# Context's rotated keys and values for the second cross-attention made earlier and kept in DRAM

## What is computed

```python
def _L1_xattn_ref(x, latents, gamma_x, beta_x, gamma_l, beta_l, Wq, Wkv, Wo):
    # x is the context (ctx_1024), latents the decoder's own tokens
    xn = layer_norm(x, gamma_x, beta_x)
    ln = layer_norm(latents, gamma_l, beta_l)
    q = (ln @ Wq).reshape(b, m, h, d)            # 8 heads of 64
    kv_x = xn @ Wkv                              # 256 -> 512 keys, 512 values
    k_x, v_x = (kv_x[..., :INNER], kv_x[..., INNER:])
    kv_l = ln @ Wkv
    ...
    k_x = rope_rotate_k(k_x)                     # k * cos + neg_half(k) * sin
    ...
    k = jnp.concatenate([k_x, k_l], axis=2)
    v = jnp.concatenate([v_x, v_l], axis=2)
    attn = jax.nn.softmax(jnp.einsum('bhid,bhjd->bhij', q, k), axis=-1)
    out = jnp.einsum('bhij,bhjd->bhid', attn, v)
    return out @ Wo
```

## Time and profile before

| | us |
|---|---|
| median of 3 runs | 1689.41 (1687.66 to 1691.91) |
| the profiled execution | 1690.37 |
| its span in the trace | 1688.5 |
| PE busy | 1427.5 (85%) |
| DVE busy | 891.1 (53%) |
| ACT busy | 583.3 (35%) |
| POOL busy | 537.5 (32%) |

### The profile page before, as it was taken

One profiled execution on the slowest core, in us unless ns is written; L12 is line 12 of the kernel. 1 busy time (PEld: TensorE's weight loads), 2 busy tenths in 40 slices (PEclk: granted clock), 3 DMA queues, 4 the chain that ended last, 5 costly groups with the idle time before them and its releaser, 6 DMA issues.

```text
span 1688.5 us, 29289 instructions
## 1 busy us (share of the span) xinstructions
PE 1427.5 (85%) x10056; PEld 1105.6 (65%) x10056; DVE 891.1 (53%) x2529; ACT 583.3 (35%) x1449; POOL 537.5 (32%) x515
## 2 busy tenths in 40 slices
PE   7667997559999999937999589998887766999987
PEld 4454676449999999914666446565555534999975
DVE  7353556531222211169875245767678842666656
ACT  4203543112121222123343124444444212666652
POOL 2002000012222223102333211134435473766775
PEclk9988999669999999977999889999999898999999
DMA  7771000068888888311000061112223699666528
GB/s 224 200 243 51 2 14 14 25 239 326 323 305 311 321 307 319 143 50 50 1 1 1 25 154 35 66 48 88 88 82 104 223 325 330 170 177 174 165 70 339
DMA packets 133602, 258.94 MB, mean 153 GB/s; under 512 B 13898, under 2 KB 106216, under 8 KB 127184
## 3 DMA queue, kind: packets, MB, share of 16 engines
q1 hardware_dynamic: 111328, 210.89, 37.7%
q0 software_dynamic: 17520, 39.88, 6.6%
q10 hardware_dynamic: 4608, 6.29, 1.1%
HBM read 197.71 MB, written 52.72 MB: 148 GB/s over the span
## 4 chain that ended last, share of the span: by engine, by line
PE 50%; issue 8%; DVE 8%; POOL 6%; DMA 5%; SPq 2%; ACT 1%; POOLq 1%; ACTq 0%; DVEq 0%
PE bank L152 46%; POOL xe L1664 4%; DMA arena<-in_banka 2%; PE bank L2208 2%; DMA arena<-yr 2%; DVE arena L1962 1%; PE bank L1079 1%; SPq L2415 1%; DVE arena L1952 1%; DVE arena L197 1%; PE bank L1233 1%; POOLq L165 1%; DVE arena L177 1%; DMA arena<-xd,arena 0%; POOL arena L190 0%
## 5 line engine op out<-in xcount | busy, mean ns | idle before, releaser
L152 PE MATMUL bank<-arena 128*128 128x128 f32 (+8 forms) x8728 | 1282.2, 336 | 149.0 <-DMA arena<-in_banka 24.4
L152 PEld LDWEIGHTS bank<-arena 128*128 128x128 f32 (+5 forms) x8728 | 962.1, 181 | 422.1 <-issue 262.0
L2349 POOL DMA_INDIRECT yr<-arena x159 | 173.3, 1090 | 89.2 <-ACT arena L2279 50.0
L1124 DVE TENSOR_SCALAR arena<-bank,arena 128x128 f32<-128x128 f32 x188 | 52.9, 344 | 279.6 <-PE bank L152 279.6
L190 POOL TENSOR_TENSOR arena<-arena 128x1 f32<-128x1 f32 (+1 forms) x48 | 37.3, 777 | 335.4 <-DVE arena L182 335.4
L1151 POOL DMA_INDIRECT arena<-xd,arena x47 | 45.8, 975 | 257.0 <-PE bank L1079 221.8
L1664 POOL DMA_INDIRECT xe<-arena x112 | 113.2, 1010 | 31.6 <-issue 31.6
L2314 DVE COPY arena<-arena 128x768 f32 x127 | 75.6, 595 | 56.8 <-issue 56.7
L1864 ACT ACTIVATE arena<-bank,arena 128x256 f32<-128x256 f32 x128 | 58.9, 472 | 97.5 <-DVE arena L1952 97.5
L1102 ACT ACTIVATE arena<-bank 128x256 f32<-128x256 f32 x47 | 18.0, 383 | 212.4 <-PE bank L152 212.4
L1111 ACT ACTIVATE arena<-bank,arena 128x128 f32<-128x128 f32 x188 | 53.6, 368 | 92.6 <-PE bank L152 92.6
(11 more groups left out here) (259 smaller groups left out, 1448.2 us busy)
## 6 DMA issues: line engine op xcount, KB each, us to landing
arena<-in_bank SPq DMA_DIRECT2D x47, 2052.0 KB
arena<-xe SPq DMA_DIRECT2D x159, 129.0 KB, 2.4
arena<-kd SPq DMA_DIRECT2D x16, 1024.0 KB, 11.0
arena<-arena SPq DMA_DIRECT2D x16, 896.0 KB, 4.4
arena<-in_bank SPq DMA_DIRECT2D x8, 1536.0 KB, 12.7
arena<-yr SPq DMA_DIRECT2D x16, 768.0 KB, 15.2
xe<-arena SPq DMA_DIRECT2D x1, 6321.0 KB, 29.0
arena<-in_ctx SPq DMA_DIRECT2D x8, 512.0 KB, 4.2
```

Of the source, the lines that this page charges most:

```text
L152: return t.matmul(o, l, r, start=start, stop=stop, skip_group_check=True)
L1124: h = v.tensor_scalar(h_ring[i % 3][:, (4 + m) * 128:(5 + m) * 128], banks[b][:, m * 128:(m + 1) * 128], sbc(w_ring[i % 5], 4100 + m), 0.0 ...
L2349: p.indirect_dma_start(yr, bass.IndirectOffsetOnAxis(ap=sidx.bitcast(I32)[:, n:n + 1], axis=0), y2_ring[n % NY], None, bounds_check=14335, ...
```

## The change

The context's keys and values for all 16 blocks are made before the second cross-attention: blocks 8 to 15 in turns 9 to 17 and in the end of the first cross-attention (that stage still holds context groups 2 and 3), blocks 0 to 7 among the steps of the mixer's first part (their context is loaded again and normalized during the first experts, turns 30 to 33 of DVE's list). Each block's 128x1024 result goes to a DRAM tensor `kxv` from ACT's queue, and the second cross-attention loads it back from SP's queue into a ring of three. The steps are `cn`, `cnd`, `cp` (norm and transposes), `ck` (keys), `cv` (values) and `ct` (transposes of the rotated keys). ACT now copies keys, values and transposed keys; POOL does the whole rotation, in three instructions. The steps `cnorm`, `cnormed`, `pc`, `kx`, `kv0` and `kt` of the second cross-attention are gone. `MIXER` is a new order also for steps that were there (group 1's `sum`, `xa`, `na` and `aff` now come before `0wo`). The core of the diff:

```diff
+        kxv = nc.dram_tensor("kxv", [2048, 1024], F32, kind="Internal").ap()
+        def tensor_kv(t, u, n, bank_of):
+            cT, i, keys, _, _ = kv_place(n)
+            if u == "ct":
+                t.wait_ge(roped, kv_turn(n) + 1)
+                b = bank_of(("ct", n))
+                for m in range(4):
+                    h = t.transpose(banks[b][:, m * 128:(m + 1) * 128], keys[:, m * 128:(m + 1) * 128], ident)
+            else:
...
+                for kc in range(2):
+                    h = mm(t, banks[b], cT[:, kc * 512 + i * 128:kc * 512 + i * 128 + 128], wcol("kv2", kc, 512 if u == "cv" else 0, 512), kc == 0, kc == 1)
+        def scalar_kv(a, u, n):
...
+            if u == "ck":
...
+                a.activation(keys, banks[b], ACT.Copy).then_inc(bank_free[b], 1)
+            else:
+                if n % 8 >= 2:
+                    a.wait_ge(kept[n % 2], 16 * (kv_turn(n) // 2))
+                a.wait_ge(bank_full[b], k + 1)
+                a.activation(both[:, 512:1024] if u == "cv" else both[:, 0:512], banks[b], ACT.Copy).then_inc(bank_free[b], 1)
+                if u == "ct":
...
+                    a.dma_start(kxv[n * 128:(n + 1) * 128, :], both).then_inc(kept[n % 2], 16)
+        def gpsimd_kv(p, n):
...
+            p.wait_ge(bank_free[b], k + 1)
+            p.tensor_tensor(view(part, 0, [[64, 8], [32, 2], [1, 32]]), view(keys, 32, [[64, 8], [-32, 2], [1, 32]]), view(cc("sin"), 0, [[0, 8], [32, 2], [1, 32]]), ALU.mult).then_inc(pstep.up(), 1)
+            p.wait_ge(pstep.sem, pstep.n)
+            p.tensor_tensor(view(keys, 0, [[64, 8], [1, 64]]), view(keys, 0, [[64, 8], [1, 64]]), view(cc("cos"), 0, [[0, 8], [1, 64]]), ALU.mult).then_inc(pstep.up(), 1)
+            p.wait_ge(pstep.sem, pstep.n)
+            p.tensor_tensor(keys, keys, part, ALU.add).then_inc(roped, 1)
...
+            context = [("ck", 8), ("cv", 8)]
+            for n in range(9, 16):
+                context += [("ck", n), ("ct", n - 1), ("cv", n)]
+            context += [("ct", 15)]
+            ln = {9: (("cn", 2),), 10: (("cnd", 2),), 11: (("cn", 3),), 12: (("cnd", 3), ("cp0", 2), ("cp1", 2)), 13: (("cp0", 3), ("cp1", 3))}
...
+                yield from itertools.islice(more, {13: 1, 14: 2, 15: 2, 16: 2, 17: 1}.get(b, 0))
                 if b < 16:
                     yield "mt", b
+                yield from itertools.islice(more, {13: 1, 14: 2, 15: 2, 16: 2, 17: 1}.get(b, 0))
...
+            after = {("ow1", 3): 2, ("lg", 2): 3, ("lg", 3): 3}
...
         def sync_bank(s):
+            for i in range(2):
+                s.wait_ge(kept[i], 64)
...
-            before = {0: ("xnorm",), 1: ("xnormed", "pl0"), 2: ("pl1", "cnorm"), 3: ("cnormed", "pc0"), 4: ("pc1", "qk0"), 5: ("qk1",), 6: ("qk2",), 7: ("qk3",)}
+            before = {0: ("xnorm",), 1: ("xnormed",), 2: ("pl0",), 3: ("pl1",), 4: ("qk0",), 5: ("qk1",), 6: ("qk2",), 7: ("qk3",)}
...
         def sync_second(s):
+            for n in range(3):
+                load_kv(s, n)
...
+            for n in range(3, 16):
+                load_kv(s, n)
+                if n >= 6 and n % 2 == 0:
+                    stage_rows(s, n // 2 - 3)
...
+        def load_kv(s, n):
+            if n >= 3:
+                b, k = U["p2", n - 3]
+                s.wait_ge(bank_full[b], k + 1)
+            s.dma_start(f_kv[n % 3], kxv[n * 128:(n + 1) * 128, :]).then_inc(kv_in[n % 3], 16)
```

More of the change, by code:

```diff
@@ L1 @@
 from contextlib import ExitStack
+import itertools
 import numpy as np
@@ L539, in steps_c @@
                 yield u, g
+                yield from itertools.islice(more, after.get((u, g), 0))
+            yield from more
         def sync_cross(s):
@@ L1204, in build @@
         e_th = [alloc(512) for _ in range(2)]
-        e_st = [alloc(64) for _ in range(12)]
+        e_st = alloc(208)
+        assert top[0] <= 48864
         summed, xa_done, xb_done, mixed, wkv_done, hh_done, squared, xi_added, x4_added, dec_done, xn_pads = (
@@ L1305, in scalar_mix @@
             for g, u in MIX:
+                if u == "cp":
+                    for kc in range(2):
+                        b, n = U["cp", g, kc]
+                        a.wait_ge(bank_full[b], n + 1)
+                        a.activation(XT[:, 1024 * g + 512 * kc:1024 * g + 512 * kc + 512], banks[b], ACT.Identity, scale=vcol("gx", kc), bias=vcol("bx", kc)).then_inc(bank_free[b], 1)
+                    continue
+                if u in ("ck", "cv", "ct"):
+                    scalar_kv(a, u, g)
+                    continue
                 xg = xrow(g)
@@ L1363, in scalar_mix @@
                     scaled_by(g, "c", xg, xg).then_inc(astep.up(), 1)
+            for i in range(2):
+                a.wait_ge(kept[i], 128)
         def gpsimd_mix(p):
@@ L1535, in build @@
         f_kl = [alloc(2048) for _ in range(2)]
-        f_kx = [alloc(512) for _ in range(2)]
-        f_v = [alloc(1024) for _ in range(3)]
-        f_rp = [alloc(1024) for _ in range(2)]
+        f_vl = [alloc(512) for _ in range(3)]
+        f_kv = [alloc(1024) for _ in range(3)]
+        alloc(1536)
         f_s = [alloc(1024) for _ in range(2)]
@@ L1602, in steps_f @@
                     yield "sd", 0
-                elif nb + 1 < 16 and not odd:
-                    yield "kx", nb + 1
                 if 0 <= i - 1 < 32:
                     yield "tr", i - 1
-                if nb + 1 < 16:
-                    if odd:
-                        yield "kt", nb + 1
-                    yield ("kv1" if odd else "kv0"), nb + 1
+                if odd and nb + 1 < 16:
+                    yield "kv1", nb + 1
                 if g + 1 < 4:
@@ L1689, in tensor_second @@
                         t.wait_ge(late_in, 64)
-                        for what in ("fpl", "fpc"):
-                            for kc in range(2):
-                                b, n = U[what, g, kc]
-                                t.wait_ge(bank_free[b], n + 1)
+                        for kc in range(2):
+                            b, n = U["fpl", g, kc]
+                            t.wait_ge(bank_free[b], n + 1)
                     lt = f_lt[g % 2]
@@ L1750, in tensor_second @@
                             t.wait_ge(bank_free[b], n + 1)
-                    for what in ("kv0", "kv1"):
-                        b, n = U[what, g]
-                        t.wait_ge(bank_free[b], n + 1)
+                    b, n = U["kv1", g]
+                    t.wait_ge(bank_free[b], n + 1)
                     b = misc_use(("p2", g))
```

199 lines of the change are left out of this document (119 added, 80 removed).

## The result

| | before | after |
|---|---|---|
| median of 6 runs, us | 1688.93 (1687.66 to 1691.91) | 1696.34 (1694.8 to 1697.49) |
| ratio, 95% interval | | 1.0037 (1.0025 to 1.005) |
| profiled execution, its span | 1690.37, 1688.5 | 1694.8, 1693.0 |

The change costs 7 us by the medians (0.4%, with the whole interval above 1) where the prediction had a gain of 36. I cut both traces at the same six places: DVE's first cast for routing, its first memset in the mixer, its first cast behind the barrier, its first and last minima of the second cross-attention, the end. The last column is what the prediction said of the difference.

The account below looks back on a forecast made before the run. PE nearly fills the second cross-attention, with PE or DVE setting different half-steps. Second cross-attention -52, first +11, experts 0, mixer +5 make -36 us from 1690.4: 1654 profiled, 1653 median; range 1632 to 1674.

Parts of the forecast that it names:

- The lead-in: Start of the second cross-attention: loses context norm, transposes, scaling and two pairs of products; 9 us less, bounds 6 and 12.
- The three groups of half-steps with projections: Second cross-attention, half-steps 4-7, 12-15, 20-23: even ones save about 4 us, odd 0.4 to 1; 25 us in all.
- the other 14 ... together 11: Remaining half-steps of the second cross-attention's loop: three gain nothing, the others 0.4 to 1.5 us each; 11 us saved.
- Half-steps 0 to 3: Second cross-attention's loop, without choice of experts: PE leads and loses 7.8 us of work; 7 us saved.
- +5, bounds -2 and +12: Mixer: POOL's rotations slow DVE by 5 to 8 us, clock and order gains offset what exceeds 5; 5 us longer.
- a share of one half to three quarters overlapped at 1.66 times: Mixer's start: part of about 16 us of two-operand SBUF work on DVE slowed beside POOL's rotations; +5 to +8 us.
- +11, bounds +5 and +18: First cross-attention: turns +12, context norms on DVE +1, end part -2; 11 us longer in all.
- I take 11: First cross-attention, turns 13 to 17: 22.9 us of added PE work, 11 of 12 free us usable; +12 us.
- The term of +5.3 for the power behind the rotation: First cross-attention's end: POOL's power for group 3's norm waits behind block 14's rotation; 5.3 us longer.
- the same products at full clock ... about 7 together: First cross-attention's end: `ow`, the transposes and `lg` run faster at full clock; about 7 us saved.
- (b): Rival, chance 0.17: placed work costs much more, first stage +22 and mixer +15; only -15 us in all, 1674.
- (c): Rival, chance 0.06: PE hides nothing, each `ct` stops it, all 66 us are paid again; +14 us, 1703.

Follow-up runs that it names:

- spare_products: Changed kernel with two spare product pairs put back on PE in seven even half-steps of the second cross-attention without projections; ratio 0.9982 to the kernel before.
- best1: Changed kernel with group 3's norm and last choice moved ahead, the mixer's rotations on DVE and the spare products; ratio 1.0014 to the kernel before, on another chip.
- rotation_out: Changed kernel with POOL's three rotation instructions left out in all 16 blocks, keys stored unrotated; median 1673.9 us, ratio 0.9909 to the kernel before.
- norm_choice_first: Changed kernel with group 3's power ahead of block 14's rotation and the last choice's exponentials ahead of three ACT copies; median 1689.8 us, ratio 1.0.

## Why the prediction was wrong, step by step

**Right.** The lead-in, -9.0. The three groups of half-steps with projections, -24.4 (predicted -25), though partly by luck: I had given each even one about 4 us, and the first of a group (4, 12, 20) gave 5.3 and the second (6, 14, 22) 1.5 to 2.3; the odd ones gave 0.1 to 0.7. Half-steps 26 and 30 near 11 us, as before. The experts, nothing. The rest of the second stage, 2 us. 512 KB loads land in 3.8 us and hold nobody.

**Loop, "the other 14 ... together 11": with half-step 30 they took 1.4 us more than before.** I had said that the products taken out of them would buy DVE's share, and had no term for PE's clock. The step that failed is the argument that taking work from PE there buys nothing or a little: it can cost. The row that should have told me is in the earlier trace rows: in half-step 30 of the kernel before, one without `kx` and `kv0`, PE "still runs at half speed" behind its 6.84 us of waiting. I read that as a reason why nothing is gained, and did not carry it to the half-steps that were about to become of this kind. 24, at a clock of 1.00 before and 0.80 after, went from 7.51 to 8.35 us; 28, from 1.00 to 0.65, from 8.11 to 9.70. spare_products shows it: 8.2 us back, 7.6 of them in these half-steps. They then stand 6.2 us below the kernel before, so of the 12.4 missed 7.6 came back with the products and the clock; the other 5 are in the 0.4 to 1.5 us that I gave a half-step for DVE's share, and no run takes them apart. best1 bounds the rule: with the clock at 1.00 but ACT's copy late, nothing came back. Half-steps 0 to 3 gave 5.1 of 7.

**Mixer, "+5, bounds -2 and +12": +14.5.** The mechanism was named, its size was not. I had the contention at +5 to +8; rotation_out puts the rotations at 18.8 us, 16 of them visible as longer DVE instructions. The order, which I had at 0 to -2, came to +3.0 at most. That leaves -7.3 for the rest, where I had 5 for the clock; no run takes it apart. The step that failed is "a share of one half to three quarters overlapped at 1.66 times": the factor came from one row, a scan of 1.20 us, and I spread it over instructions a third and two thirds as long. By the rows above what a DVE instruction pays is about 1.0 us whatever its own length: a scaling 0.41 to 1.42, a product 0.75 to 1.76, a scan 1.20 to 2.21. So the price goes by the count of DVE instructions that meet a rotation, not by their time. And "DVE work with two operands from SBUF" left the scalings out. Of the Trainium skill I had drawn only on contention with two inputs. The Trainium skill (SBUF — State Buffer, section Who interferes with whom) has another case too: `tensor_scalar` and copies can enter a mode that takes the shared pair of ports, and the second to issue is blocked until the first is done. The trace agrees: 5.34 us for four scalings beside four instructions of POOL.

**First cross-attention, "+11, bounds +5 and +18": +25.3.** Turns, predicted +12 and +1 for the norms: the `mt` of block 15 came 12.1 us later (304.0 instead of 291.9) and the two turns behind it took 4.9 more (17.7 instead of 12.8 to `ot0`). 4.1 of the 12.1 came up to the `mt` of block 13, with the norms, which I had at 1, and the `cp` transposes, which I had in the 12; 7.9 came in one turn, from the `mt` of block 14 to that of block 15 (16.2 us instead of 8.3), where four context steps stand. PE is busy 31.0 of 34.9 us there at a clock of 1.00 (before 22.7 of 31 at 0.84); less of its waiting could be used than I took, "I take 11" of 12. End part, predicted -2: +8.3 (32.6 instead of 24.4 from `ot0` to routing). The term of +5.3 for the power behind the rotation was right (3.15 us from statistics to scaling before, 8.37 now). Wrong were "the same products at full clock ... about 7 together", which gave 3, and what I did not look for: ACT's queue, where the exponentials of the last choice stand behind three copies that wait for PE, 5.2 us; another 1.0 is the scaling beside POOL. norm_choice_first shows both hand-overs, and that in its profile only 3.3 us of them could be had, since the moved work then stands before the barrier.

**The rivals.** (b) was nearest in the first three stretches and named rotations and DVE slowing each other; its +22 and +15 are +25.3 and +14.5. It kept the second stage at -52, which was -37, and -35 with the rest. None of the three misses (14, 10 and 15 us) would have made the change slower by itself; I had priced none of them together with another that came from somewhere else. (c) named the sign, for another reason than the one that held: PE's added work in the mixer cost nothing once the rotations were gone (238.9 us).

What stays open: how much of the cross-attention's +17 in the turns is PE's bare load and how much its order, why the spare products gave 8.2 and 10.9 us on one chip and 1.0 on the other, and what the -7.3 in the mixer is made of. No run took these apart.

## What to carry to other kernels

Before work is put "into idle time" of one engine, list what it brings to each of the others in that stretch: here PE had the room, and some 16 us were paid by DVE beside a POOL that had been idle. Before work is taken from PE, look at the granted clock of the stretch that remains: where the chain is another engine's, PE's spare work may be what keeps it fast (it was on one chip, and hardly on the other). A hand-written order belongs to a placement; the same new order was 12.7 us better or 7 worse depending on which engine made the rotation.

## What was not expected of the hardware

- A DVE instruction beside one of POOL's rotations paid about 1.0 us, whatever its own length: 0.41 to 1.42 us for a 128x256 scaling, 0.75 to 1.76 for a 128x512 product, 1.20 to 2.21 for a scan, 0.22 to 1.25 for a product of 128x64. POOL's instructions grew less, from 1.27 to 1.6 or 1.7 us beside the 128x512 products. Reciprocals (3.35 us) and products with one operand in a bank (0.68) did not change.
- Spare products in PE's waits made a loop shorter: 24 us of them, -8.2 us, with the granted clock of half-step 24 at 1.00 instead of 0.80 and of half-step 28 at 1.00 instead of 0.65; on another chip, with the clock at 1.00 as well, only -1.0 us.
- Two chips differed by 60 us in the same kernel before (1689 and 1750). In the changed kernel 56 of it lie in the second experts (375 and 431 us) and 4 in the loop, with the ratios to the kernel before alike (1.0037 and 1.0062).
